# Row sums of attention 2's second head group: four key tiles added on VectorE and GpSimd, then multiplied with ones

## The chip, the cores and the metric

The kernel runs on one core of a Trainium2 chip. The metric is the device time of one execution in microseconds (us), lower is better. Engines as the profile names them: PE is TensorE (matmuls; PEld is its weight load), DVE is VectorE, ACT is ScalarE, POOL is GpSimd, SP is SyncE, which here only issues DMAs.

## The reference, cut to what matters

A batch of 16 sequences, T = 512 queries, width 256, context S = 1601 keys. Per sequence: a first cross attention with 16 heads and a layer norm, a Mamba block with its chunked scan, and a second cross attention with 8 heads of width 32:

```
q = (xn @ Wq).reshape(b, Lq, 8, 32);  k = (enc @ Wk)...;  v = (enc @ Wv)...
scores = einsum('bqhd,bkhd->bhqk', q, k) / sqrt(32)      # 8 heads x 512 queries x 1601 keys
p = softmax(where(pad_mask, -1e9, scores), axis=-1)
out = resid + einsum('bhqk,bkhd->bqhd', p, v) @ Wo
```

The kernel computes softmax as exp(score - maximum) and divides by the row sum at the end. The row sum of each query and head, over 1601 keys, is what the change touches.

## The kernel before

One loop over the 16 sequences, written out by hand for every engine; semaphores order the engines and each engine runs its instructions strictly in program order. Keys are cut into KT = 13 tiles of 128 (the last holds 65). Heads are taken in groups of GH = 4: attention 1 has G0 = 4 groups (gi = 0 to 3), attention 2 has G1 = 2 (gi = 4 and 5). In all texts "step t" is one round of the loop over t in `group`, "tile t" the key tile t.

In step t of a group of attention 2, TensorE computes the scores of tile t with keys on partitions: four matmuls of 512 columns (L1042), two heads ("half 0"), then two more ("half 1"). ScalarE takes the exponential of each half into `PR[:, t % 2]` (L1470; two buffers of four heads x 512 floats). Then `times_v` runs for tile t - 1: four matmuls that give each head 32 columns of the array, PR times V into PSUM bank 6 (L1067), and four of the same form that multiply PR with ones into bank 7 (L1072). The latter are the row sums, accumulated in PSUM over the 13 tiles. At the group's end ScalarE copies bank 7 to `rs` and bank 6 to `ctxn`; for the first group VectorE divides (`divide`) during step 0 of the second.

Between these matmuls TensorE takes entries of another piece of work, attention 1 of the next sequence: raw scores (L992, banks 4 and 5 in turn) that VectorE adds the mask to and reduces to a maximum (L1671, two instructions), and four projections of keys called "back" (L954), which ScalarE takes out (L1425 and L1428) ahead of its exponentials of the same step and GpSimd splits into three parts (L752, L755, L758). A table, `beside`, places the entries in six slots of a step: slots 0 to 3 behind the four score matmuls, slot 4 between V and the ones, slot 5 at the end. In the second group the four "back" entries are in slot 4 of steps 6 to 9. An entry's bank is free when VectorE (or ScalarE) is done with the entry two before it (`left`): TensorE waits for that in place. VectorE goes through the same slots in the same order. Raw entries of step 5 and later read `kst` and `qst`, which SP loads with 12 DMAs once the first group is done (L565, L568).

## Time and profile before

| | us |
|---|---|
| median of 3 runs | 8260.42 (8257.19 to 8279.29) |
| profiled execution, whole | 8254.75 |
| its span, first to last instruction | 8252.8 |
| TensorE busy | 7493.3 (91%) |
| VectorE busy | 5271.3 (64%) |
| ScalarE busy | 3415.3 (41%) |
| GpSimd busy | 1930.5 (23%) |
| matmuls with ones, L1072: 3328, busy | 444.4 |
| mean granted TensorE clock | 0.968 |

The table comes from the page of the profiled execution. Busy times are averages over stages that are limited by different engines, and a matmul's end is modelled: two matmuls that follow each other overlap in the rows, so what one costs TensorE is read from the distance between starts. The stretch from 3651 to 3718 us is the second head group of attention 2 in one of the 16 sequences.

### The profile page before, as it was taken

What the parts mean: (1) busy time and instruction counts of PE and PEld (TensorE: products, weight loads), DVE (VectorE), ACT (ScalarE), POOL (GpSimd) and SP (SyncE); (2) the same over time, 40 slices, a digit from 0 to 9 for tenths busy, and PEclk for the clock granted to TensorE, in tenths of its full rate; (3) what the DMA queues carried; (4) which work ended last, traced back from release to release, by engine and by line L of the source; (5) the groups of instructions that cost most, each with busy time, mean ns of one, the idle gap of its engine ahead of it and who ended that gap; (6) DMA issues with size and microseconds to landing.
All of it is one profiled execution on the core that took longest, in us unless ns stands there. A gap on an engine that the chain in (4) does not pass through costs nothing.

```text
span 8252.8 us, 130448 instructions
## 1 busy us (share of the span) xinstructions
PE 7493.3 (91%) x37924; PEld 3455.1 (42%) x38244; DVE 5271.3 (64%) x12637; ACT 3415.3 (41%) x4310; POOL 1930.5 (23%) x1928
## 2 busy tenths in 40 slices
PE   3999999999999999999999999999999999999999
PEld 0353443535334353443534335343343534435344
DVE  3676666766666675666765667666676666667656
ACT  0434435344353434535344353443534345343443
POOL 3041130402204031130401304022040311404113
PEclk6999999999999999999999999999999999999999
DMA  3142240423314142231422304233141322314223
GB/s 75 28 80 43 38 70 15 83 39 54 60 22 79 31 70 52 37 61 25 83 40 42 67 15 83 39 52 61 21 80 32 64 51 32 68 31 79 44 38 65
DMA packets 244583, 423.17 MB, mean 51 GB/s; under 512 B 38745, under 2 KB 154363, under 8 KB 243593
## 3 DMA queue, kind: packets, MB, share of 16 engines
q1 hardware_dynamic: 241751, 413.22, 29.0%
q8 instruction: 367, 6.01, 0.3%
q14 instruction: 417, 3.42, 0.1%
q10 hardware_dynamic: 2048, 0.53, 0.0%
HBM read 191.17 MB, written 8.54 MB: 24 GB/s over the span
## 4 chain that ended last, share of the span: by engine, by line
PE 73%; DVE 11%; issue 7%; ACT 4%; DMA 2%; SPq 1%; POOL 1%; DVEq 1%; ACTq 0%; POOLq 0%
PE ps L1067 13%; PE ps L992 11%; PE ps L954 8%; PE ps L1037 7%; PE ps L1040 6%; PE ps L1014 4%; DVE mx L1700 4%; PE ps L1072 4%; PE ps L1042 3%; ACT PR L1470 2%; PE ps L1222 2%; PE ps L1105 2%; PE ps L1278 2%; DVE ps L1735 1%; PE ps L1306 1%
## 5 line engine op out<-in xcount | busy, mean ns | idle before, releaser
L1470 ACT ACTIVATE PR<-ps 128x1024 f32<-128x1024 f32 x2496 | 2502.0, 1024 | 2449.1 <-PE ps L1040 1355.0
L1671 DVE CUSTOM_DVE_ANT_0 ps<-ps,maskq 128x402 f32<-128x402 f32 x4203 | 2405.6, 587 | 1452.1 <-PE ps L992 1320.1
L1067 PE MATMUL ps<-PR,vbuf 128*32 128x512 f32 x9984 | 1333.7, 606 | 7.5 <-ACT PR L1470 2.5
L992 PE MATMUL ps<-kst,qst 96*128 96x402 bf16 (+1 forms) x3115 | 1016.6, 340 | 126.1 <-DVE mx L1671 97.8
L1040 PE MATMUL ps<-maskk,identb 128*128 128x512 bf16 x2592 | 985.0, 380 | 0.0
L1700 DVE TENSOR_REDUCE mx<-ps 128x2 f32<-128x804 f32 x1024 | 932.8, 985 | 63.0 <-PE ps L1014 59.9
L1037 PE MATMUL ps<-qst,kst 99*128 99x512 bf16 x2496 | 916.8, 381 | 12.5 <-ACT PR L1470 5.2
L1014 PE MATMUL ps<-kst,qst 100*128 100x402 f32 x2688 | 733.1, 397 | 108.5 <-DVE mx L1700 107.7
L1042 PE MATMUL ps<-qst,kst 102*128 102x512 f32 x1664 | 728.3, 498 | 73.1 <-ACT PR L1470 70.8
L992 PEld LDWEIGHTS ps<-kst,qst 96*128 96x128 bf16 x3115 | 280.2, 97 | 1227.7 <-DVE mx L1671 856.0
L766 POOL MEMSET kst<- 96x252 f32 (+1 forms) x34 | 8.7, 255 | 3044.7 <-PE ps L1067 2997.8
L1014 PEld LDWEIGHTS ps<-kst,qst 100*128 100x128 f32 x2688 | 456.3, 194 | 367.0 <-DVE mx L1700 341.8
L1671 DVE DVE_READ_ACCUMULATOR2_ANT mx<- 128x1 f32 x4203 | 591.9, 141 | 0.0
L1735 DVE TENSOR_TENSOR ps<-ps,maskk 128x1024 f32<-128x1024 f32 x208 | 256.4, 1233 | 413.3 <-PE ps L1037 413.3
L727 POOL TENSOR_SCALAR maskk<-stage 128x512 bf16<-128x512 int32 (+1 forms) x238 | 428.5, 1801 | 330.4 <-DMA stage<-in_maskt 323.7
L992 PE MATMUL ps<-KS,QS 96*128 96x402 bf16 x1088 | 384.4, 354 | 112.0 <-DVE mx L1671 82.6
L954 PE MATMUL ps<-ctxs,wk_s 128*128 128x402 f32 (+1 forms) x1056 | 459.8, 562 | 24.7 <-ACT rest L1428 23.7
L727 POOL TENSOR_SCALAR maskq<-stage 128x402 bf16<-128x402 int32 (+1 forms) x272 | 427.8, 1573 | 192.4 <-DMA stage<-in_mask 169.6
L1072 PE MATMUL ps<-PR,ones 128*32 128x512 f32 x3328 | 444.4, 606 | 0.0
L1037 PEld LDWEIGHTS ps<-qst,kst 99*128 99x128 bf16 x2496 | 243.7, 98 | 416.6 <-ACT PR L1470 190.2
L1425 ACT ACTIVATE khl<-ps,cols 128x402 bf16<-128x402 f32 (+1 forms) x136 | 81.1, 596 | 796.7 <-PE ps L954 796.7
L954 PE MATMUL ps<-wv_s,ctxs 128*128 128x256 f32 (+1 forms) x1664 | 408.7, 380 | 0.0
(200 smaller groups left out, 8235.8 us busy)
## 6 DMA issues: line engine op xcount, KB each, us to landing
kst<-khl SPq DMA_DIRECT2D x300, 200.1 KB, 7.5
stage<-in_maskt SPq DMA_DIRECT2D x204, 256.0 KB
stage<-in_mask SPq DMA_DIRECT2D x204, 201.0 KB
kst<-khl SPq DMA_DIRECT2D x96, 402.0 KB, 8.6
kst<-khl SPq DMA_DIRECT2D x96, 398.5 KB, 11.1
ctxs<-in_ctxt SPq DMA_DIRECT2D x17, 1601.0 KB, 17.6
qst<-q1hl SPq DMA_DIRECT2D x192, 128.0 KB, 4.5
win_s<-in_w_in SPq DMA_DIRECT2D x16, 1288.0 KB, 5.7
```

Source lines behind the costliest of these rows:

```text
L727: nc.gpsimd.tensor_scalar(dst, stage[0:rows, n % 2, 0:w], 0.0, MASKED, ALU.is_equal, ALU.mult)\
L954: mm = pe.matmul(o, l, r, start=(k == 0), stop=(k == DT - 1))
L992: pe.matmul(ps[:, bank, 0:w], QS[gi][0:KROWS, h, i * P:(i + 1) * P], KS[gi][0:KROWS, h, c0:c0 + w], start=True, stop=True).then_inc(s_raw, 1)
L1014: mm = pe.matmul(ps[:, bank + e, 0:CW], QS1[g][0:MROW1 + 1, h, i * P:(i + 1) * P], KS1[g][0:MROW1 + 1, h, cc[e]:cc[e] + CW], start=True, s ...
L1037: mm = pe.matmul(o, KS[gi][0:SROWS, h, t * P:(t + 1) * P], QS[gi][0:SROWS, h, :], start=True, stop=(h in added))
L1040: mm = pe.matmul(o, identb[:, :], maskk[:, t, :], start=False, stop=True)
L1042: mm = pe.matmul(o, KS1[gi - G0][0:SROWS1, h, t * P:(t + 1) * P], QS1[gi - G0][0:SROWS1, h, :], start=True, stop=True)
L1067: mm = pe.matmul(ps[32 * j:32 * j + 32, 6, :], l, PR[:, t % 2, j, :], start=(t == 0), stop=(t == KT - 1), tile_position=(0, 32 * j))
L1072: mm = pe.matmul(ps[32 * j:32 * j + 32, 7, :], ones[:, 0:32], PR[:, t % 2, j, :], start=(t == 0), stop=(t == KT - 1), tile_position=(0, 32 ...
L1470: nc.scalar.activation(PR[:, t % 2, 2 * half:2 * half + 2, :], ps[:, bank:bank + 2, :], ACT.Exp, scale=scale).then_inc(s_p, 1)
L1671: nc.vector.tensor_tensor_reduce(src, src, maskq[:, i, c0:c0 + w], 1.0, -3.0e38, ALU.add, ALU.max, mx[:, c, h * QT + i:h * QT + i + 1]).th ...
L1700: nc.vector.tensor_reduce(mx[:, 2 * c:2 * c + 2, h * QT + i], ps[:, bank:bank + 2, 0:CW], AX.X, ALU.max)\
```

## The change

`SEGMENTS` tells for each head group of attention 2 over how many key tiles a sum is formed before it meets the ones. In the first group it is one tile each, as before. In the second it is 4, 4, 4 and 1: the probabilities of tiles 0 to 3 are added elementwise, those of tiles 4 to 7 and 8 to 11 too, and each sum is multiplied with ones once; tile 12 goes directly. So of 13 quads of L1072 in that group 4 remain. VectorE adds heads 0 and 1 (`add01`, one instruction of 128x1024 a tile, into `sum01`, part of `ctxn`), GpSimd adds heads 2 and 3 (`add23`, two instructions of 128x512 a tile, into `sum2` and `rs`). There are nine adds on each side, for tiles 1, 2, 3, 5, 6, 7, 9, 10 and 11; the first of a segment adds tiles t - 1 and t. ScalarE waits for the adds before it overwrites a buffer of PR. `add01` stands in slot 4 of step t on VectorE, `add23(t)` in a new loop over t on GpSimd in which the parts of the "back" entries of steps t + 1 and t + 2 follow the add of an odd t.

```diff
+        SEGMENTS = [[1] * KT, [4] * (KT // 4) + [1]]
...
 POOL
+                def add23(g, t):
+                    m = b * len(ADDS) + ADD_COUNT[g, t] - 1
+                    pool.wait_ge(s_p, b * 2 * NG * KT + ((G0 + g) * KT + t) * 2 + 2)
+                    if FIRST_ADD[g, t]:
+                        pool.wait_ge(s_addread, LEAD + b * len(ADDED) + sums_read(g, t))
+                        pool.wait_ge(s_norm, LEAD + b * NG + G0 + g)
+                    else:
+                        pool.wait_ge(s_add23, 2 * m)
+                    alone(pool)
+                    for j, dst in ((2, sum2[:, :]), (3, rs[:, :])):
+                        other = PR[:, (t - 1) % 2, j, :] if FIRST_ADD[g, t] else dst
+                        nc.gpsimd.tensor_tensor(dst, other, PR[:, t % 2, j, :], ALU.add).then_inc(s_add23, 1)
...
-                for item in BACK:
-                    parts(b + 1, item)
+                for t in range(KT):
+                    if (1, t) in ADD_COUNT:
+                        add23(1, t)
+                    for step in (t + 1, t + 2) if t % 2 else ():
+                        for j in BACK_STEPS.get(step, ()):
+                            parts(b + 1, BACK[j])
...
 PE, times_v
                 if gi >= G0:
+                    here = (gi - G0, t)
+                    if here not in DIRECT and t < KT - 1:
+                        mm.then_inc(s_pv, 1)
                     between(t + 1, 4)
-                    for j in range(GH):
-                        mm = pe.matmul(ps[32 * j:32 * j + 32, 7, :], ones[:, 0:32], PR[:, t % 2, j, :],
-                                       start=(t == 0), stop=(t == KT - 1), tile_position=(0, 32 * j))
-                mm.then_inc(s_pv, 1)
+                    if here in DIRECT:
...
+                    elif here in ADDED:
+                        assert t < KT - 1
+                        pe.wait_ge(s_add01, b * len(ADDS) + ADD_COUNT[here])
+                        pe.wait_ge(s_add23, 2 * (b * len(ADDS) + ADD_COUNT[here]))
+                        for j, src in enumerate((sum01[:, 0, :], sum01[:, 1, :], sum2[:, :], rs[:, :])):
+                            mm = pe.matmul(ps[32 * j:32 * j + 32, 7, :], ones[:, 0:32], src,
+                                           start=(here == ENDS_OF[gi - G0][0]), stop=False, tile_position=(0, 32 * j))
+                        mm.then_inc(s_addread, 1)
...
 ACT, exponentials
+                        if gi >= G0 and t >= 2:
+                            g = gi - G0
+                            read = adds_until(g, t - 1 if FIRST_ADD.get((g, t - 1)) else t - 2)
+                            if read and half == 0:
+                                act.wait_ge(s_add01, b * len(ADDS) + read)
+                            elif read:
+                                act.wait_ge(s_add23, 2 * (b * len(ADDS) + read))
...
 DVE
+            def add01(b, g, t):
+                dve.wait_ge(s_p, b * 2 * NG * KT + ((G0 + g) * KT + t) * 2 + 1)
+                if FIRST_ADD[g, t]:
+                    dve.wait_ge(s_addread, LEAD + b * len(ADDED) + sums_read(g, t))
+                    other = PR[:, (t - 1) % 2, 0:2, :]
+                else:
+                    dve.wait_ge(s_add01, b * len(ADDS) + ADD_COUNT[g, t] - 1)
+                    other = sum01
+                nc.vector.tensor_tensor(sum01, other, PR[:, t % 2, 0:2, :], ALU.add).then_inc(s_add01, 1)
...
+                        if slot == GH and (gi - G0, t) in ADD_COUNT:
+                            add01(b, gi - G0, t)
```

What moves in the order of the instructions is shown at three places. VectorE, second group, end of step 7 and start of step 8, before. "ISA ps,mx" and "ISA mx" together are one raw entry (mask and maximum); the 396 wide one is slot 0 of step 8:

```order
L1671 ISA ps,mx<-ps,maskq 128x402
L1671 ISA mx 128x1
L1659 REGISTER_ALU
L1671 ISA ps,mx<-ps,maskq 128x402
L1671 ISA mx 128x1
L1659 REGISTER_ALU
L1671 ISA ps,mx<-ps,maskq 128x396
L1671 ISA mx 128x1
```

The same place in the changed kernel:

```order
L1746 ISA ps,mx<-ps,maskq 128x402
L1746 ISA mx 128x1
L1805 REGISTER_ALU
L1810 REGISTER_ALU
L1812 TENSOR_TENSOR ctxn<-ctxn,PR 128x1024
L1734 REGISTER_ALU
L1746 ISA ps,mx<-ps,maskq 128x402
L1746 ISA mx 128x1
L1734 REGISTER_ALU
L1746 ISA ps,mx<-ps,maskq 128x396
L1746 ISA mx 128x1
```

The add of tile 7, with its two waits, now stands between the entry of slot 3 and that of slot 5.

TensorE, end of step 8 (V of tile 7, the third "back" projection, the sums, slot 5), before:

```order
L1067 MATMUL ps<-PR,vbuf 32x512 x4
L968 REGISTER_ALU
L954 MATMUL ps<-ctxs,wk_s 128x402 x2
L1072 MATMUL ps<-PR,ones 32x512 x4
L968 REGISTER_ALU
L992 MATMUL ps<-kst,qst 128x396
```

and in the changed kernel (sum_61 is `sum2`):

```order
L1120 MATMUL ps<-PR,vbuf 32x512 x4
L1021 REGISTER_ALU
L1007 MATMUL ps<-ctxs,wk_s 128x402 x2
L1135 REGISTER_ALU
L1136 REGISTER_ALU
L1138 MATMUL ps<-ctxn,ones 32x512 x2
L1138 MATMUL ps<-sum_61,ones 32x512
L1138 MATMUL ps<-rs,ones 32x512
L1021 REGISTER_ALU
L1045 MATMUL ps<-kst,qst 128x396
```

The four matmuls with ones stay here, but now behind waits for VectorE's and GpSimd's sums; in steps 1, 2, 3, 5, 6, 7, 9, 10 and 11 they are gone.

GpSimd, second group, behind the parts of the fourth "back" entry (395 wide), before:

```order
L755 CAST khl<-rest 128x395
L756 REGISTER_ALU
L758 TENSOR_TENSOR khl<-rest,khl 128x395
L918 ISA
L762 MEMSET kst 96x4x63
```

and in the changed kernel:

```order
L783 CAST khl<-rest 128x395
L784 REGISTER_ALU
L786 TENSOR_TENSOR khl<-rest,khl 128x395
L941 REGISTER_ALU
L943 REGISTER_ALU
L950 TENSOR_TENSOR sum_61<-PR 128x512
L950 TENSOR_TENSOR rs<-PR 128x512
L941 REGISTER_ALU
L946 ISA
L950 TENSOR_TENSOR sum_61<-sum_61,PR 128x512
L950 TENSOR_TENSOR rs<-rs,PR 128x512
```

The adds of tiles 9, 10 and 11 follow the last parts; those of tiles 6 and 7 stand in the same way behind the parts of the second "back" entry, ahead of those of the third.

## Rows read from the trace of the kernel before

**Rows 1.** Page, part 1: busy us (share of the span) xinstructions
```profile
PE 7493.3 (91%) x37924; PEld 3455.1 (42%) x38244; DVE 5271.3 (64%) x12637; ACT 3415.3 (41%) x4310; POOL 1930.5 (23%) x1928
```
**Rows 2.** Timeline of PE (start us, us, ..., idle before <-releaser), steps 1 and 5
```profile
3655.88 1.04 PE L1072 MATMUL ps<-PR,ones 128*32 128x512 f32 x8
3656.85 0.50 PE L1042 MATMUL ps<-qst,kst 102*128 102x512 f32 x1
...
3667.76 0.34 PE L992 MATMUL ps<-kst,qst 96*128 96x402 bf16 x1 [0.52 <-DMA qst<-qhl]
```
**Rows 3.** Source view, L992: what its engine waited for (us, times)
```profile
  DMA qst<-qhl: 6.5, 11
```
**Rows 4.** Timeline of PE, steps 7 and 8 of the second group
```profile
3682.71 1.62 PE L954 MATMUL ps<-ctxs,wk_s 128*128 128x402 f32 x4
3684.26 1.07 PE L1072 MATMUL ps<-PR,ones 128*32 128x512 f32 x8
...
3686.42 0.51 PE L1042 MATMUL ps<-qst,kst 102*128 102x512 f32 x1 [0.81 <-ACT PR L1470]
...
3687.18 0.34 PE L992 MATMUL ps<-kst,qst 96*128 96x402 bf16 x1
...
3688.76 1.07 PE L1067 MATMUL ps<-PR,vbuf 128*32 128x512 f32 x8
3689.75 1.62 PE L954 MATMUL ps<-ctxs,wk_s 128*128 128x402 f32 x4
```
**Rows 5.** Timeline of ACT, step 7
```profile
3684.37 0.60 ACT L1425 ACTIVATE khl<-ps,cols 128x402 bf16<-128x402 f32 x1 [4.12 <-PE ps L954]
...
3685.34 1.94 ACT L1470 ACTIVATE PR<-ps 128x1024 f32<-128x1024 f32 x2
```
**Rows 6.** Waits of the whole span: us, times, longest
```profile
PE ps L1042 <- ACT PR L1470: 70.8, 96, 1.0
```
**Rows 7.** Windows: us, busy of each engine (x), PEclk, DMA share, GB/s
```profile
3681.00:3688.00 7.00, 6.06 (x31) 2.03 (x31) 3.04 (x11) 2.91 (x4) 2.34 (x4) 1.00 0.00 1
3702.00:3707.00 5.00, 4.79 (x28) 1.59 (x28) 3.71 (x13) 2.36 (x3) 0.26 (x1) 1.00 0.68 101
...
3564.00:3568.00 4.00, 2.75 (x10) 1.26 (x9) 3.93 (x7) 1.08 (x2) 3.71 (x3) 1.00 0.20 51
3568.00:3572.00 4.00, 3.77 (x10) 2.29 (x9) 4.00 (x5) 0.00 (x0) 3.69 (x4) 0.52 0.20 54
```
**Rows 8.** Timeline of DVE, steps 0, 7, 10 and 11
```profile
3655.92 0.69 DVE L1726 TENSOR_TENSOR ctxn<-ctxn,rs 128x512 f32<-128x512 f32 x1
...
3685.75 0.58 DVE L1671 CUSTOM_DVE_ANT_0 ps<-ps,maskq 128x402 f32<-128x402 f32 x1 [3.08 <-PE ps L992]
...
3704.31 0.58 DVE L1671 CUSTOM_DVE_ANT_0 ps<-ps,maskq 128x402 f32<-128x402 f32 x1 [0.63 <-PE ps L992]
...
3709.23 0.58 DVE L1671 CUSTOM_DVE_ANT_0 ps<-ps,maskq 128x396 f32<-128x396 f32 x1 [0.63 <-PE ps L992]
```
**Rows 9.** Timeline of DVE, two operations with both operands in SBUF, in the Mamba block
```profile
3457.52 2.38 DVE L1840 SCALAR_TENSOR_TENSOR xc<-th,xc 128x512 f32<-128x512 f32 x1
...
3497.00 1.21 DVE L1860 TENSOR_TENSOR windows<-windows,GM 128x1024 f32<-128x1024 f32 x1
...
3501.05 0.69 DVE L1917 TENSOR_TENSOR ug<-ug,zs 128x512 f32<-128x512 f32 x1
```
**Rows 10.** Timeline of POOL at the same places
```profile
3457.01 2.34 POOL L829 TENSOR_TENSOR aU<-aa,upto 128x1024 f32<-128x1024 f32 x1
...
3497.24 1.87 POOL L857 TENSOR_TENSOR dx<-dx,dec 128x512 f32<-128x512 f32 x1 [4.13 <-DVE dx L1895]
3499.07 1.04 POOL L864 TENSOR_TENSOR Hst<-Hst,dec 128x512 f32<-128x512 f32 x1
```
**Rows 11.** Timeline of POOL, step 7 of the second group
```profile
3685.60 0.90 POOL L752 TENSOR_TENSOR rest<-rest,khl 128x402 f32<-128x402 f32 x1 [4.38 <-ACT rest L1428]
3686.62 0.52 POOL L755 CAST khl<-rest 128x402 bf16<-128x402 f32 x1
3687.29 0.95 POOL L758 TENSOR_TENSOR khl<-rest,khl 128x402 bf16<-128x402 f32 x1
```

More of the change, by code:

```diff
@@ L474, in xattn_mamba, with adds_until, sums_read @@
         NMX = 4
+        SEGMENTS = [[1] * KT, [4] * (KT // 4) + [1]]
+        assert all(sum(x) == KT for x in SEGMENTS)
+        ADDS, ENDS = [], []
+        for g, lengths in enumerate(SEGMENTS):
+            t = 0
+            for n in lengths:
+                ADDS += [(g, t + i, i == 1) for i in range(1, n)]
+                t += n
+                ENDS.append((g, t - 1, n > 1))
+        ADD_COUNT = {(g, t): n + 1 for n, (g, t, _) in enumerate(ADDS)}
+        FIRST_ADD = {(g, t): is_first for g, t, is_first in ADDS}
+        ENDS_OF = [[(h, t) for h, t, _ in ENDS if h == g] for g in range(G1)]
+        ADDED = [(g, t) for g, t, several in ENDS if several]
+        DIRECT = [(g, t) for g, t, several in ENDS if not several]
+        def adds_until(g, t):
+            return max([ADD_COUNT[x] for x in ADD_COUNT if x[0] == g and x[1] <= t], default=0)
+        def sums_read(g, t):
+            return sum(x < (g, t) for x in ADDED)
         def head_bank(gi, t, half):
@@ L909, in _ @@
                     n += 1
+                def add23(g, t):
[11 more added lines that the diff above has]
+                for t in range(KT):
+                    if (0, t) in ADD_COUNT:
+                        add23(0, t)
+                    if t % 2:
+                        for n in range(n, min(n + 2, NPIECE)):
+                            piece(n)
+                        n = min(n + 1, NPIECE)
                 for n in range(n, NPIECE):
@@ L1162, in whole_decays @@
                 mm.then_inc(s_dps, 1)
-            for first in (s_pv, s_yp):
+            for first in (s_pv, s_yp, s_addread):
                 pe.nop(nofuse=True).then_inc(first, LEAD)
```

14 lines of the change are left out of this document (added).

## The prediction

> **What bounds the kernel now.** I read the page first, then the timeline of each engine over the second head group of attention 2 (3651 to 3718 us), then the waits and windows. The page makes TensorE look like the bound: busy 91% of the span, the next engine 64% [rows 1]. By that, a quad of ones that disappears is a pure gain. A quad costs TensorE the distance from its start to the next matmul's, 3656.85 - 3655.88 = 0.97 us [rows 2]. Nine quads a sequence and 16 sequences give 9 x 0.97 x 16 = 140 us, the most that the change can bring. So the question is which of those nine places TensorE really sets. The reader is to see three kinds of steps.
>
> Steps 0 to 4 are short and end in a DMA: the first raw entry of step 5 starts at 3667.76 after 0.52 us of idle time that a load of `qst` ended [rows 2]. The same wait stands in 11 of the 16 sequences, 6.5 us in all, with the same size each [rows 3]. That load depends on the end of the first group, not on this one, so TensorE arriving earlier only waits longer.
>
> Steps 6 to 9 hold a "back" projection. In step 7 it starts at 3682.71 [rows 4]; ScalarE can take it out only when it is done, at 3684.37, and its exponential of half 0 starts at 3685.34 [rows 5]; the scores of step 8 need that and start at 3686.42, after 0.81 us of idle time on TensorE [rows 4]. The quad of ones (3684.26 to about 3685.3) lies beside ScalarE's part. From one projection to the next it is 7.04 us (3682.71 to 3689.75) [rows 4]. Such waits of scores for ScalarE occur 96 times, six a sequence, 70.8 us [rows 6].
>
> Steps 10 to 12 look bound by TensorE (4.79 us busy of 5.00), but VectorE is busy 3.71 us there [rows 7]. A step is 3709.23 - 3704.31 = 4.92 us [rows 8]; VectorE has 4.92 - 3.71 = 1.21 us left.
>
> **Durations of the added work.** VectorE's add, 128x1024 with both operands in SBUF: 1.21 us, from the same form in the Mamba block [rows 9]. GpSimd's, 128x512: 1.04 us with nothing beside it [rows 10]; two of them and the wait ahead of them, 2.2 us a tile. Beside each other they aren't independent. GpSimd's L857, of the same 128x512 as L864, takes 1.87 instead of 1.04 us: it starts at 3497.24 while VectorE's L1860 runs until 3498.21, and 1.87 - 1.04 = 0.83 is nearly what was left of it [rows 9, 10]. The other way round, VectorE's L1840 takes 2.38 us (a 128x512 with two operands in SBUF takes 0.69): it starts at 3457.52, in the middle of a GpSimd operation that ends at 3459.35 [rows 9, 10]. So I let whoever comes second wait for the instruction of the first. The Trainium skill says the same (SBUF — State Buffer, "Who interferes with whom"): a VectorE instruction with two SBUF inputs contends with a GpSimd instruction that reads SBUF, and the second blocks fully. The trace agrees; without that rule my sum below would be 62 us, with it 92.
>
> **The change, place by place** (one sequence; then times 16).
>
> Removed quads. Tiles 0, 1, 2 (steps 1 to 3): 0, the DMA takes it. Tiles 5, 6, 8 (steps 6, 7, 9): 0, they lay beside ScalarE's 2 us. Tiles 4, 9, 10 (steps 5, 10, 11): TensorE saves 0.97 a step, but VectorE gets 1.21 more in the same step and has 1.21 left, so the raw entries, each of which waits for VectorE's entry two before, go on at the old pace of about 4.9 us: 0, between -0.1 and +0.1 each.
>
> Adds, steps 1 to 4: +0.4. VectorE's add of tile 1 comes after the division (ends 3656.61 [rows 8]) and ends at 3657.8; GpSimd's pair waits for the same division and then for that add, so it runs to 3660.0. ScalarE may overwrite the buffer only then; its half 1 of step 2 ends at 3661.1. The pair of tile 2 follows with VectorE's add of tile 3 between its two halves (61.2 to 64.5), then tile 3 (64.6 to 66.7). TensorE's first quad of sums runs until 67.8, and the first raw entry of step 5 comes at 68.2 instead of 67.76. Bounds: 0 (the adds never meet) to 1.5 (each GpSimd add costs 1.87).
>
> Adds in "back" steps: +1.15 each for tiles 6, 7 and 9, together 3.45. This is the largest term. VectorE's add stands ahead of slot 5's entry and waits for the exponential of its tile. In step 7 that ends just ahead of the scores it releases, about 3686.4 [rows 4], while slot 5's entry was done by 3686.4, from 3685.75 on [rows 8]. Now the add runs from 3686.4, behind GpSimd's L752 that ends at 3686.50 [rows 11], to 3687.7, the entry until 3688.35. The raw entry of slot 1 in step 8 needs that entry's bank: it started at 3687.18 [rows 4] and now starts at 3688.4. All that is queued behind it moves: two score matmuls, V, the next projection, which sets the chain of the next step. VectorE idled there before (3.08 us ahead of slot 5's entry [rows 8]), but the idle time is ahead of the exponential and the add can't use it. Bounds: 0 to 1.3 each.
>
> The sums in step 8: +0.5. GpSimd splits the second projection first (3685.60 to 3688.24 [rows 11], +1.15 for the shift, +1.1 for VectorE's add in between: 3690.5), then adds tiles 6 and 7 (4.4 us: 3694.95). TensorE, 2.3 us later than before, is through with its third projection at 3693.6, waits 1.4 us, and the quad and slot 5's entry end at 3696.25; ScalarE would have released the next scores at 3695.75. Bounds 0 to 1.5.
>
> VectorE behind GpSimd in steps 10 and 11: +0.9 and +0.5. GpSimd's adds of tiles 9, 10 and 11 come in one row after the fourth projection's parts; VectorE's add of tile 10 meets the second half of tile 9's (0.9), that of tile 11 perhaps one more (half of 1.04). VectorE has nothing left there, so it counts. Bounds 0 to 2.2 together.
>
> Sum: 0.4 + 3.45 + 0.5 + 1.4 = 5.75 us a sequence, times 16 = 92 us. Against the profiled execution's 8254.75 us (span 8252.8, 2 us around it) that is 8347; the median of the runs lies 6 us above the profiled one. I say 8350. The low bounds (only the "back" steps at 0.85, nothing else) give 41 us, 8296; the high ones 1.5 + 3.9 + 1.5 + 2.2 = 9.1, 146 us, 8400.
>
> **Rivals.**
>
> A. TensorE is the bound after all. The savings in steps 1 to 3, 5, 10 and 11 count, 6 x 0.97 = 5.8 us, and the adds find VectorE idle: 16 x 5.8 = 93 us less, 8160. For it: the 91%, and VectorE's idle time of 1.21 us a step. Against it: the DMA's 0.52 us, which decides the first three, and the place of the add behind the exponential. It decides from the point at which the add ends before the entry of slot 1 is asked for; the numbers miss that by 1.2 us three times a sequence.
>
> B. The adds hide better than I think, for instance because TensorE had 0.81 us of slack in each "back" step that takes part of the shift: 3 x 0.4 + 0.5 = 1.7 us, 27 us, 8282. Against it: the stall is on the far side of that slack, behind the scores' start.
>
> C. TensorE's clock falls. In this group the granted clock is 1.00 with TensorE busy 6.06 of 7.00 us [rows 7]. Elsewhere it fell to 0.52 right after four microseconds with 2.75 us busy, 69% [rows 7]. In steps 6 to 9 the changed kernel leaves 0.81 + 0.97 + 1.15 = 2.9 us idle of 8.2, 65% busy, in two gaps close together; steps 1 to 4 have a gap of 2 us too. A stretch at 1.2 GHz instead of 2.4 GHz over half a step's 5 us of matmuls costs about 2.5 us; once or twice a sequence 40 to 80 us on top: 8390 to 8430. The Trainium skill (TensorE: Matmul & The Clock Gate, "What's actually happening") says that activity alone releases the throttle, and so speaks against a change that takes matmuls away; no row here shows this group below 1.00.
>
> **How the numbers follow.** Forecast 0.62, C 0.22, B 0.07, A 0.05, and no visible change 0.04 (every term near its low bound). A measurement of this kernel tells about 0.3%, 25 us, from no change. Faster: A, 0.05, and a little of the rest, 0.06. Same: 0.04 and a part of B, 0.06. Slower 0.88. Range: from the low bounds to the middle of C, 8295 to 8415; that leaves out A, part of B and the upper half of C.
>
> **What the profile of the changed kernel would show.** Right: the ones quads of this group at 4 x 16 instead of 13 x 16; the first raw entry of step 5 still about where the load of `qst` puts it; from one "back" projection to the next 8.2 us instead of 7.04 behind steps 6 and 7; in steps 7, 8 and 10 raw entries of slot 1 waiting more than 1 us for VectorE; waits of TensorE for GpSimd's sums once in step 8; VectorE's adds longer than 1.21 us where GpSimd runs; the group 5 to 7 us longer than 66; all else unchanged. Wrong: step 5 starting 3 us earlier (A), slot 1's entry without a wait (B), a granted clock of 0.5 in the group (C).

## The result, and the profile after

The changed kernel takes 8400.80 us, median of 4 runs (8399.85 to 8401.66); the kernel before, run beside it on the same chip, 8258.81 (8249.94 to 8279.29, 4 runs). The ratio is 1.0168, 95% interval 1.0149 to 1.0187: 142 us more, 8.9 us a sequence. The forecast was 92 us more, 8350, with a range of 8295 to 8415. Direction and range hold; the size does not.

The page of the changed kernel, span and part 1 (as [rows 1]):

```profile
span 8399.9 us, 130033 instructions
PE 7541.8 (90%) x37092; PEld 3464.3 (41%) x37092; DVE 5482.3 (65%) x12781; ACT 3413.7 (41%) x4310; POOL 2381.8 (28%) x2216
```

TensorE has 832 matmul records fewer: 1152 with ones are gone, as the change has it, and 320 more stand for the mask matmuls of attention 1 (`maskk,identb`), which the change leaves alone and of which the record of before lacks some. So the 48.5 us more of busy time can't be taken as they are; without the mask matmuls in both they are 17.5 us. Even that is more time for fewer matmuls. Its mean granted clock, the share of full speed that the chip let it run at, went from 0.968 to 0.946. The lines of the kernel that answer for the change, with the shortest, the median and the longest of one instruction in ns (the ones over single tiles that stay, then VectorE's adds, then two of GpSimd's four groups of adds):

```profile
L1129 PE MATMUL ps<-PR,ones x1792: 592/592/617, 605.1 to 8389.3; 128*32 128x512 f32 x200
...
L1812 DVE TENSOR_TENSOR ctxn<-ctxn,PR x96: 1218/1429/2225, 662.9 to 8381.5; 128x1024 f32<-128x1024 f32 x96
...
L950 POOL TENSOR_TENSOR sum<-sum,PR x96: 1259/1276/2084, 665.3 to 8381.7; 128x512 f32<-128x512 f32 x96
...
L950 POOL TENSOR_TENSOR sum<-PR x48: 1262/2062/2120, 660.6 to 8373.8; 128x512 f32<-128x512 f32 x48
```

The diff asks for 9 x 16 = 144 adds of VectorE and twice as many of GpSimd; the rows above are 96 of the former and half of the latter. Their shortest are 1.22 and 1.26 us.

The timeline of TensorE over steps 6 to 8 of one sequence's second group, where [rows 4] showed 7.04 us from one projection to the next:

```profile
3742.64 1.87 PE L1120 MATMUL ps<-PR,vbuf 128*32 128x512 f32 x8
3744.44 2.47 PE L1007 MATMUL ps<-ctxs,wk_s 128*128 128x402 f32 x4
...
3748.99 0.50 PE L1095 MATMUL ps<-qst,kst 102*128 102x512 f32 x1 [1.91 <-ACT PR L1545]
...
3750.89 0.51 PE L1045 MATMUL ps<-kst,qst 96*128 96x396 bf16 x1 [0.82 <-DVE mx L1746]
...
3752.91 1.94 PE L1120 MATMUL ps<-PR,vbuf 128*32 128x512 f32 x8
3754.77 2.42 PE L1007 MATMUL ps<-ctxs,wk_s 128*128 128x402 f32 x4
...
3765.07 2.39 PE L1007 MATMUL ps<-ctxs,wk_s 128*128 128x402 f32 x4
```

The reader is to see three things. From projection to projection it is 3754.77 - 3744.44 = 10.33 us, then 10.30. Where a wait of 0.81 us for ScalarE stood, it is 1.91: the 0.97 of the removed quad has become idle time of about its length, not a shorter step. And the matmuls themselves are longer: those of V take 1.87 to 1.94 us where they took 1.07, the projection 2.4 to 2.5 where it took 1.62. The windows over the same steps and over steps 10 to 12 say why (busy of each engine, then the granted clock):

```profile
3744.00:3755.00 11.00, 8.26 (x26) 2.95 (x23) 4.24 (x11) 2.91 (x4) 3.25 (x3) 0.66 0.00 1
3755.00:3765.00 10.00, 7.30 (x21) 2.44 (x21) 4.24 (x11) 2.91 (x4) 5.84 (x6) 0.67 0.00 0
3765.00:3773.00 8.00, 7.13 (x34) 2.59 (x31) 2.98 (x10) 2.91 (x4) 4.77 (x5) 0.90 0.00 1
3784.00:3796.00 12.00, 10.15 (x67) 3.02 (x66) 8.32 (x27) 5.18 (x6) 5.08 (x5) 1.00 0.84 94
```

The clock is 0.66 of full in step 6, so it stood at 1.2 GHz for about two thirds of that stretch, against 1.00 in [rows 7]. This was rival C. The Trainium skill (TensorE: Matmul & The Clock Gate, "What's actually happening") says that activity releases the throttle; this trace agrees, with 1.00 before and 0.66 after nine quads were taken away and the waits for the adds put in.

VectorE and GpSimd, first two adds of the group and the add of step 6, each engine's timeline:

```profile
3722.79 1.22 DVE L1812 TENSOR_TENSOR ctxn<-PR 128x1024 f32<-128x1024 f32 x1
...
3725.28 2.18 DVE L1812 TENSOR_TENSOR ctxn<-ctxn,PR 128x1024 f32<-128x1024 f32 x1 [0.71 <-ACT PR L1545]
...
3749.06 1.23 DVE L1812 TENSOR_TENSOR ctxn<-ctxn,PR 128x1024 f32<-128x1024 f32 x1 [5.56 <-ACT PR L1545]
3750.20 0.58 DVE L1746 CUSTOM_DVE_ANT_0 ps<-ps,maskq 128x402 f32<-128x402 f32 x1
```
```profile
3723.02 2.11 POOL L950 TENSOR_TENSOR sum<-PR 128x512 f32<-128x512 f32 x1 [4.76 <-DVE ctxn L1801]
3725.11 1.26 POOL L950 TENSOR_TENSOR rs<-PR 128x512 f32<-128x512 f32 x1
```

In step 6 the add waits 5.56 us for the exponential, then runs 1.23 us, and slot 5's entry starts only at 3750.20; TensorE's entry of slot 1, at 3750.89, is behind it. So VectorE's idle time is of no use to the add, as forecast. The first rows show the two engines in each other's way. The waits that these leave in the whole span (us, times, longest):

```profile
PE ps L1045 <- DVE mx L1746: 213.2, 510, 45.2
...
PE ps L1095 <- ACT PR L1545: 146.9, 120, 1.9
```

The second was 70.8 us in 96 waits [rows 6]; the first, in the kernel before:

```profile
PE ps L992 <- DVE mx L1671: 180.4, 469, 45.2
```

All of the loss is in the second group. The table below is worked out from the timelines: the distance from one V (the weighted sum of a key tile) to the next, mean of the 16 sequences, in us; column 6 is the distance that ends at V of tile 6, and column 0 counts from the last V of the first group. "1.2 GHz" is the time in the group at the lower clock level. The clock falls in some sequences and not in others, so a column can also be read where it stood at 1.00 throughout; texts below say "with the clock up" for that. The first group, attention 1 and the blocks between stay within about 1 us a sequence in the changed kernel. Names of the experiments are those used further down.

```
                   0    1    2    3    4    5    6     7    8    9    10   11   12   group  1.2 GHz
before           5.61 3.66 3.58 3.16 4.70 4.92 7.04  7.04 7.04 7.01 4.92 4.92 2.54  66.16    1.1
after            5.60 2.31 4.85 3.45 6.04 4.54 9.06  9.65 8.53 8.39 5.44 4.62 3.04  75.52   24.3
fill             5.62 3.45 3.93 3.16 5.34 4.93 8.23  8.95 8.59 7.95 5.65 4.92 2.54  73.27    7.0
adds_only        5.64 3.33 3.95 3.16 5.41 4.93 8.20  9.14 8.65 7.95 5.53 4.93 2.54  73.35    6.4
quads_only       5.61 2.68 2.48 2.30 7.97 5.18 7.46  8.50 7.44 7.63 4.75 4.18 2.54  68.73   16.0
quads_back       5.62 3.86 3.58 3.16 4.62 4.93 7.48  8.37 8.21 7.67 5.19 4.92 2.54  70.14   11.5
pool_only        5.60 3.15 3.57 3.14 4.87 4.91 7.03  7.03 9.53 7.01 4.91 4.91 2.54  68.22    3.0
dve_only         5.65 3.83 3.57 3.16 4.56 4.91 8.30  8.46 8.28 8.05 6.00 4.91 2.54  72.23    8.8
seg_mid          5.60 3.16 3.58 3.16 4.91 4.55 8.53 10.30 8.79 7.01 4.93 4.93 2.54  71.99   13.2
late             5.62 2.96 4.76 2.68 9.40 4.91 7.24  7.10 9.07 7.44 6.63 4.93 3.34  76.08   17.9
late_order_fill  5.62 3.55 4.92 3.26 8.76 5.35 7.04  7.13 7.13 7.01 6.69 5.16 3.35  74.96    8.3
mix_fill         5.63 3.65 3.87 3.16 5.22 4.93 7.04  7.03 7.86 7.02 8.83 6.20 2.54  72.99    9.6
mix              5.68 3.35 3.78 2.64 6.87 4.85 7.64  8.02 8.15 7.44 8.44 5.19 2.54  74.60   24.1
first_group      5.60 3.16 3.58 3.16 9.61 6.06 7.05  7.42 7.03 7.00 4.92 4.92 2.54  72.07    7.7
```

### The profile page after: what moved, and what is told of

Read it like the earlier page. It is cut to its first block, busy times and chain, and to the rows that moved or that the text cites. A ratio compares the mean times of both kernels' runs of the same rounds, so it can differ in the third digit from the quotient of the medians.

```text
span 8399.9 us, 130033 instructions
## 1 busy us (share of the span) xinstructions
PE 7541.8 (90%) x37092; PEld 3464.3 (41%) x37092; DVE 5482.3 (65%) x12781; ACT 3413.7 (41%) x4310; POOL 2381.8 (28%) x2216
## 4 chain that ended last, share of the span: by engine, by line
PE 73%; DVE 12%; issue 8%; ACT 3%; POOL 1%; DVEq 1%; DMA 1%; SPq 0%; ACTq 0%; POOLq 0%
PE ps L1120 13%; PE ps L1045 11%; PE ps L1007 8%; PE ps L1090 7%; PE ps L1093 6%; PE ps L1067 5%; DVE mx L1775 4%; PE ps L1095 4%; PE ps L1129 3%; ACT PR L1545 2%; PE ps L1290 2%; PE ps L1173 2%; PE ps L1346 2%; PE ps L1374 1%; DVE ps L1821 1%
## 5 line engine op out<-in xcount | busy, mean ns | idle before, releaser
L1120 PE MATMUL ps<-PR,vbuf 128*32 128x512 f32 x9984 | 1394.4, 632 | 7.4 <-ACT PR L1545 2.5
L1045 PE MATMUL ps<-kst,qst 96*128 96x402 bf16 (+1 forms) x3115 | 1041.8, 351 | 142.1 <-DVE mx L1746 130.3
L1093 PE MATMUL ps<-maskk,identb 128*128 128x512 bf16 x2912 | 1106.5, 380 | 0.0
L1095 PE MATMUL ps<-qst,kst 102*128 102x512 f32 x1664 | 788.0, 534 | 149.8 <-ACT PR L1545 146.9
L1007 PE MATMUL ps<-ctxs,wk_s 128*128 128x402 f32 (+1 forms) x1056 | 484.6, 588 | 23.2 <-ACT rest L1496 22.2
L1095 PEld LDWEIGHTS ps<-qst,kst 102*128 102x128 f32 x1664 | 332.3, 208 | 317.4 <-ACT PR L1545 235.3
## 6 DMA issues: line engine op xcount, KB each, us to landing
ctxs<-in_ctxt SPq DMA_DIRECT2D x17, 1601.0 KB, 17.5
```

The lines of the kernel that those rows point to most:

```text
L1007: mm = pe.matmul(o, l, r, start=(k == 0), stop=(k == DT - 1))
L1045: pe.matmul(ps[:, bank, 0:w], QS[gi][0:KROWS, h, i * P:(i + 1) * P], KS[gi][0:KROWS, h, c0:c0 + w], start=True, stop=True).then_inc(s_raw, 1)
L1093: mm = pe.matmul(o, identb[:, :], maskk[:, t, :], start=False, stop=True)
L1095: mm = pe.matmul(o, KS1[gi - G0][0:SROWS1, h, t * P:(t + 1) * P], QS1[gi - G0][0:SROWS1, h, :], start=True, stop=True)
L1120: mm = pe.matmul(ps[32 * j:32 * j + 32, 6, :], l, PR[:, t % 2, j, :], start=(t == 0), stop=(t == KT - 1), tile_position=(0, 32 * j))
```

## Experiments

Two theories stood against each other after the result. The add theory: all of the loss comes from the adds and their waits, and the removed quads are worth nothing. The clock theory: part of it comes because TensorE's work went away. Times are medians; "before" is the kernel before, measured beside each; ratios carry their 95% interval.

### fill: quads with zero weights where the quads of ones went

```
+                    elif t in range(KT):
+                        for j in range(GH):
+                            pe.matmul(ps[32 * j:32 * j + 32, 7, :], zeros[:, :], PR[:, t % 2, j, :],
+                                      start=(t == 0), stop=False, tile_position=(0, 32 * j))
```

> The changed kernel, and in the place of each of the nine removed quads of ones a quad with weights of zero over the same tile of PR, so that TensorE does as many matmuls as before; every wait and every add stays. Theory 1 (stalls: VectorE's add ahead of slot 5's entry, GpSimd's sums late in step 8, adds behind each other) gives 5.75 us a sequence with the clock at 1.00 in this group. Theory 2 (the clock, which fell in this group in every sequence of the changed kernel, makes up the rest of the measured 8.9 us a sequence) expects this kernel to be FASTER than the changed one although it does more: 8259 + 92 = 8350 us, 8340 to 8365, mean clock back near 0.968. If the clock is only a companion of the stalls, the quads cost nothing or something: 8400 or more, clock 0.95.

8368.21 (8363.56 to 8371.58, 4 runs) against before 8256.43 (9 runs): 1.0135 (1.0118 to 1.0152). Nine more quads a sequence than the changed kernel, and 32.6 us faster; the slowest of its runs is 28 us below the fastest of the changed kernel's, and the intervals of the two ratios only just touch (1.0149 and 1.0152). Time at 1.2 GHz in the group fell from 24.3 to 7.0 us a sequence. TensorE, steps 6 to 9 of one sequence:

```profile
3736.75 0.34 PE L1047 MATMUL ps<-kst,qst 96*128 96x396 bf16 x1 [0.98 <-DVE mx L1752]
...
3747.65 1.87 PE L1122 MATMUL ps<-PR,vbuf 128*32 128x512 f32 x8
3749.45 2.46 PE L1009 MATMUL ps<-ctxs,wk_s 128*128 128x402 f32 x4
...
3752.19 0.62 PE L1140 MATMUL ps<-ctxn,ones 128*32 128x512 f32 x2 [0.28 <-POOL rs L952]
...
3756.34 1.06 PE L1122 MATMUL ps<-PR,vbuf 128*32 128x512 f32 x8
...
3762.82 0.34 PE L1047 MATMUL ps<-kst,qst 96*128 96x402 bf16 x1 [0.90 <-DVE mx L1752]
...
3764.28 1.06 PE L1122 MATMUL ps<-PR,vbuf 128*32 128x512 f32 x8
```

The measured 8368 lies just above the expected 8340 to 8365. The raw entry behind an add waits 0.90 to 0.98 us, and where the clock stays up the step is 3764.28 - 3756.34 = 7.94 us, 0.9 more than 7.01. In step 8 of this sequence V of tile 7 and the projection behind it take 1.87 and 2.46 us, at 1.2 GHz; TensorE then comes late to GpSimd's sums and waits only 0.28 us for them.

### adds_only: adds and waits stay, all 13 quads of ones stay too, the sums are not used

```
-                        for j, src in enumerate((sum01[:, 0, :], sum01[:, 1, :], sum2[:, :], rs[:, :])):
-                            mm = pe.matmul(..., ones[:, 0:32], src, ...)
+                        for j in range(GH):
+                            mm = pe.matmul(..., ones[:, 0:32], PR[:, t % 2, j, :], ...)
```

> Adds and all their waits as in the changed kernel, but the row sums of the second group by 13 quads of ones over PR as before (the sums of four tiles are formed and not used; TensorE still waits for them in steps 4, 8 and 12). Theory 1 and 2 together: the stalls alone, clock kept, about 8350 us, and within 15 us of the kernel with zero weights, since both keep 13 quads. If instead the removed quads had brought something in steps 5, 10 and 11 (0.97 us each), the difference between this and before would be larger, up to 8259 + 16 x (5.75 + 2.9) = 8397.

8374.43 (8371.85 to 8375.74, 4 runs): 1.0144 (1.0127 to 1.0161), the same as fill step by step in the table. That the filling quads have zero weights is not what helps; that TensorE has the work is. It is above the expected 8350 and within 15 us of fill, as expected.

This run also shows what the adds and waits cost with the clock up, since in one sequence the clock stays at 1.00 from step 2 to the group's end. Step 8 there, TensorE's timeline and the window:

```profile
699.62 1.06 PE L1120 MATMUL ps<-PR,vbuf 128*32 128x512 f32 x8
...
704.43 1.06 PE L1138 MATMUL ps<-PR,ones 128*32 128x512 f32 x8 [2.20 <-POOL rs L950]
...
708.08 1.06 PE L1120 MATMUL ps<-PR,vbuf 128*32 128x512 f32 x8
```
```profile
699.62:708.08 8.46, 5.98 (x31) 1.98 (x30) 2.99 (x11) 2.91 (x4) 6.65 (x7) 1.00 0.01 3
```

TensorE waits 2.20 us for GpSimd and the step takes 8.46 us, 1.42 more than 7.04. In 13 of the other 14 sequences, with 3.4 us at 1.2 GHz, it takes 8.7: the slower matmuls stand where the wait stood. The other columns with the clock up are 8.06, 8.07 and 7.95 (6, 7 and 9), 26.39 for columns 0 to 5 together against 25.36 before, and 13.00 for 10 to 12 against 12.39; fill has the same values wherever its clock stays up, which it never does in column 8.

### quads_only: the same nine quads go from the kernel before, nothing is added

Row sums of nine tiles are left out.

```
+                    keep = gi == G0 or t % 4 == 3 or t == KT - 1
-                    for j in range(GH):
+                    for j in range(GH) if keep else ():
```

> The kernel before with the quads of ones of tiles 0-2, 4-6 and 8-10 of the second group left out, nothing added; the row sums of that group then miss those tiles. Theory 1: steps 1-3 end in the load, steps 6, 7 and 9 in ScalarE; steps 5, 10 and 11 have VectorE busy only 3.71 of 4.92 us, so there the quads do pay without the adds: up to 3 x 0.97 us a sequence, 8259 - 47 = 8212 us. Theory 2 takes from that what the lower clock costs in steps 6 to 9, where TensorE then idles 1.8 us of 7: V, back projection and scores at 1.2 GHz add about 2 us to each step that is hit, so 8212 to 8300. The rival that TensorE sets the steps: 9 x 0.97 x 16 = 140 us less, 8120.

8310.57 (8289.08 to 8317.55, 4 runs): 1.0057 (1.0038 to 1.0077), above the 8212 to 8300 of the theory with the clock. Less work and nothing in its place, and the kernel is slower by 54 us. Waits of the whole span:

```profile
PE ps L992 <- DMA qst<-qhl: 46.6, 16, 3.3
```

Columns 1 to 3 are 2.9 us shorter and column 4 is 3.3 longer: TensorE comes early and waits for the load of `qst`, in all 16 sequences. That is the DMA claim of the prediction. Columns 6 to 9 grow by 2.9 us together with no add anywhere; they have 7.6 of the group's 16.0 us of low clock, and where the clock stays up they take 7.04 or less, as before. Columns 10 to 12 are 0.9 us shorter, 1.5 with the clock up: there the removed quads do pay.

### quads_back: only the three quads of tiles 5, 6 and 8 go

Their row sums are left out.

```
+                    keep = gi == G0 or t not in (5, 6, 8)
```

> The kernel before with three quads of ones left out, those of tiles 5, 6 and 8 (steps 6, 7 and 9 of the second group); nothing is added, and the row sums of that group miss these tiles. Place-by-place theory without the clock: the three quads lie beside ScalarE, so the time stays 8255, within 10 us. Theory with the clock: with TensorE idle 1.8 us instead of 0.8 in each of these steps the granted clock falls to 1.2 GHz in some of them, and what is left of the work takes twice as long there: 1 to 2 us a sequence SLOWER by removing work, 8270 to 8290. Rival (TensorE sets the steps): 3 x 0.97 x 16 = 47 us faster, 8208.

8349.42 (8330.93 to 8354.93, 5 runs) against 8266.45 (8250.8 to 8289.92, 9 runs): 1.0091 (1.0072 to 1.0109). Three quads a sequence that lay beside ScalarE's work were left out, and it costs 83 us, more than expected, and more than quads_only lost with nine. Windows of one sequence, the end of step 4 to step 8:

```profile
4237.00:4247.00 10.00, 9.57 (x55) 3.22 (x54) 6.16 (x24) 3.99 (x4) 0.00 (x0) 1.00 0.07 8
4247.00:4254.00 7.00, 4.97 (x21) 1.88 (x21) 2.92 (x11) 2.92 (x4) 2.36 (x3) 0.98 0.01 2
4254.00:4263.00 9.00, 7.09 (x22) 2.61 (x21) 3.09 (x10) 2.91 (x4) 2.36 (x3) 0.69 0.00 1
4263.00:4272.00 9.00, 8.06 (x31) 2.62 (x29) 2.96 (x11) 2.91 (x4) 2.33 (x3) 0.76 0.00 0
```

At a clock of 0.98 the 7 us of step 6 hold 4.97 us of work, and the step takes 7.3: little is lost yet. Then the clock is 0.69, the same matmuls need 7.09 us, and the step takes 9.3. Of the 6.3 us a sequence that this profiled execution is longer than that of before, 4.0 lie in the group, 64 us in all; the other 2.3 lie in the stretches around it, where nothing was changed. They can't be put down to the quads: the profiled executions of the other kernels differ from that of before by -18 to +32 us in the same unchanged stretches, this one by +37.

### pool_only and dve_only: one engine's adds at a time

In each, two of the four heads are added as in the change and the other two meet the ones tile by tile. The cores of the edits:

```
pool_only
-                            add01(b, gi - G0, t)
+                        for j in range(2):
+                            pe.matmul(..., ones[:, 0:32], PR[:, t % 2, j, :], ...)
dve_only
-                    if (1, t) in ADD_COUNT:
-                        add23(1, t)
+                        for j in (2, 3):
+                            pe.matmul(..., ones[:, 0:32], PR[:, t % 2, j, :], ...)
```

> Only GpSimd adds (heads 2 and 3, with all its waits); heads 0 and 1 meet the ones tile by tile, two matmuls in each step, which take as long as four since the four run side by side. VectorE's adds are gone. Theory 1: the three stalls of 1.15 us and the meetings of the two engines go; left is TensorE's wait for the sums in step 8, 1.2 to 1.5 us a sequence with GpSimd's adds at 1.27 us: 8259 + 22 = 8281 us, 8265 to 8290, clock near 0.968. If GpSimd's adds and its place behind the projections' parts were the main cost, 8340 or more.

> Only VectorE adds (heads 0 and 1, with all its waits); heads 2 and 3 meet the ones tile by tile, so TensorE has two matmuls in each step, as long as four; GpSimd's adds are gone. Theory: the wait of slot 1's raw entry in steps 7, 8 and 10 (V6, V7, V9 late by 1.15 to 1.2 us each) stays, the wait of step 8 for GpSimd and the meetings go: 3.5 us a sequence, 8255 + 56 = 8311 us, 8295 to 8330. With the one for GpSimd alone (2.5 us a sequence, 43 us) this should add up to about the 112 us of the kernel with zero weights. Rival: the two need each other, each alone costs little: 8280.

GpSimd's alone: 8299.37 (8289.01 to 8324.35, 6 runs), 1.0058 (1.004 to 1.0075), more than the expected 8265 to 8290. VectorE's alone: 8369.52 (8358.52 to 8388.48, 4 runs), 1.0124 (1.0101 to 1.0147), more than expected. GpSimd costs one place: column 8 grows by 2.5 us, since TensorE waits for the sums there,

```profile
3716.76 0.63 PE L1137 MATMUL ps<-PR,ones 128*32 128x512 f32 x2 [2.30 <-POOL rs L950]
```

and columns 6, 7 and 9 are as before, although half of each quad went. In 14 of the 16 sequences the clock falls in column 8 as well; in the two others the column is 8.55, so 1.5 us are the wait and the rest is the clock. With VectorE's adds columns 6 to 10 grow by 1.3, 1.4, 1.2, 1.0 and 1.1. Columns 8 and 10 do so by the clock alone: where it stays up they are 7.04 (one sequence) and 4.91 (five), as before, against 8.06, 8.07 and 7.94 for columns 6, 7 and 9. V of tile 7, which begins column 8, takes 1.94 us in one of the others:

```profile
3741.88 1.94 PE L1116 MATMUL ps<-PR,vbuf 128*32 128x512 f32 x8
```

So in step 8 a wait for GpSimd with the clock up, or TensorE at 1.2 GHz, each make the step longer, and with both it is hardly longer than with one (8.46 and 8.7 us in adds_only).

### seg_mid: one segment of four, tiles 4 to 7, the rest direct

```
-        SEGMENTS = [[1] * KT, [4] * (KT // 4) + [1]]
+        SEGMENTS = [[1] * KT, [1] * 4 + [4] + [1] * 5]
```

> The second group's segments are 1,1,1,1,4,1,1,1,1,1: only tiles 4 to 7 are added, on both engines; the other nine tiles meet the ones directly, so steps 0 to 4 and 10 to 12 are as before. Theory (place by place): the steps up to the third 'back' projection carry most of the cost: V6, V7 and V8 late by 1.2, 1.2 to 1.9 and 1.5 us, plus the clock, which can fall since three quads are missing in steps 5 to 7: 4 to 6 us a sequence, 8257 + 80 = 8337 us, 8320 to 8355. Rival (the cost is spread evenly over the nine adds): 3/9 of 144 us, 8305.

8336.95 (8329.85 to 8350.5, 4 runs) against 8253.65 (7 runs): 1.0112 (1.0069 to 1.0154). Three adds instead of nine, and 83 us of the 142 are there; columns 6 to 8 take 6.5 us more, all others together 0.7 less. The number that was expected, 8337, came, but in part by luck: columns 6, 7 and 8 are late by 1.5, 3.3 and 1.8 us where 1.2, 1.2 to 1.9 and 1.5 were expected with the clock to come on top, and the profiled execution is 18 us shorter than that of before in stretches that were not changed.

### late: VectorE adds tile t in the next step

The add no longer stands between the exponential and the entry of slot 5.

```
-                        if slot == GH and (gi - G0, t) in ADD_COUNT:
-                            add01(b, gi - G0, t)
+                        if slot == GH and (gi - G0, t - 1) in ADD_COUNT:
+                            add01(b, gi - G0, t - 1)
```

> The changed kernel with VectorE's add of tile t moved one step on, to slot 4 of step t + 1, where VectorE is idle before ScalarE's exponential; all else as in the changed kernel. Theory 1: the wait of slot 1's raw entry for VectorE in steps 7, 8 and 10 goes (1.15 us each, 3.45 a sequence, 55 us); the clock still falls, since the quads are still missing: 8401 - 55 = 8346 us, 8325 to 8370. If the place of the add isn't what costs: 8395 or more.

8440.81 (8418.97 to 8446.11, 4 runs): 1.0227 (1.0182 to 1.0272). It missed the expected 8346 by almost 100 us. Columns 6 and 7 did fall back to 7.24 and 7.10. But the sums of step 4 now come late (column 4: 9.40).

### late_order_fill: the same, GpSimd's parts ahead of its adds, zero quads

```
+                    for j in BACK_STEPS.get(t, ()):
+                        parts(b + 1, BACK[j])
                     if (1, t) in ADD_COUNT:
                         add23(1, t)
```

> As the kernel with the late add, and two more edits: zero-weight quads keep TensorE's work (clock), and GpSimd splits a 'back' projection in its own step and adds that step's tile right behind it (before, the adds of tiles 6 and 7 stood behind the parts of the second projection). All three costs that I name are taken away while every add stays; only what steps 1 to 4 lose and what VectorE lacks in steps 10 and 11 is left: 0.8 + 0.7 us a sequence in the kernel with zero weights, 24 us: 8257 + 24 = 8281 us, 8262 to 8300. If the three causes don't exhaust the cost, it stays above 8320.

8413.31 (8405.82 to 8418.62, 4 runs): 1.0196 (1.0153 to 1.0238), against 8281 expected, again a miss. Columns 6 to 9 are 7.01 to 7.13, as before: an add away from that place costs those steps nothing. What it costs is ahead of them. VectorE and TensorE in step 4:

```profile
4245.37 2.22 DVE L1817 TENSOR_TENSOR ctxn<-ctxn,PR 128x1024 f32<-128x1024 f32 x1
...
4248.80 1.19 DVE L1721 SCALAR_TENSOR_TENSOR mrest<-mxr,nm 128x16 f32<-128x16 f32 x1
...
4250.42 1.23 DVE L1817 TENSOR_TENSOR ctxn<-ctxn,PR 128x1024 f32<-128x1024 f32 x1
```
```profile
4251.78 1.07 PE L1139 MATMUL ps<-ctxn,ones 128*32 128x512 f32 x2 [2.90 <-DVE ctxn L1817]
```

Tile 3's add is queued behind the computation of the group's maxima, of which one operation of 0.18 us takes 1.19 behind GpSimd, and TensorE stands still for 2.90 us at the sums.

### mix_fill and mix: late adds only for tiles 5, 6, 7 and 9, with and without zero quads

```
+                            for u in (t - 1, t):
+                                if (gi - G0, u) in ADD_COUNT and (u < t) == (u in (5, 6, 7, 9)):
+                                    add01(b, gi - G0, u)
```

> All adds on both engines; VectorE's adds of tiles 5, 6, 7 and 9 in slot 4 of the step after, the others in their own step; GpSimd splits a 'back' projection in its own step, then adds; zero-weight quads keep TensorE's work. From the steps measured in the two kernels it joins: V0 to V4 as with zero weights (21.5 us), V5 to V9 as with the late add (about 33.3), V10 to V12 about 13.4: 68.2 us for the group against 66.16 before, 2 us a sequence, 8255 + 33 = 8288 us, 8272 to 8305. If the late adds only moved their cost to another place, 8340 or more.

> The same without the zero-weight quads: the changed kernel's work with the adds placed where they do not stop the raw entries. If the removed quads pay once the stalls are gone: below 8255 + 33 = 8288 us and perhaps at 8255. With the clock theory: the quads' absence lets the clock fall in steps 6 to 9, as in the kernel with quads left out and nothing added (54 us slower than before): 8310 to 8345, slower than with zero-weight quads.

mix_fill: 8367.58 (8364.79 to 8371.02, 4 runs), 1.012 (1.0101 to 1.0139), expected 8288. mix: 8406.11 (8378.17 to 8421.93, 4 runs), 1.0155 (1.0131 to 1.018), expected 8310 to 8345. In mix_fill columns 6, 7 and 9 are 7.02 to 7.04 again and the cost has moved to column 10 (8.83), where tile 9's late add and tile 10's own now meet in one slot:

```profile
4268.82 2.27 DVE L1817 TENSOR_TENSOR ctxn<-PR 128x1024 f32<-128x1024 f32 x1
...
4272.34 1.23 DVE L1817 TENSOR_TENSOR ctxn<-ctxn,PR 128x1024 f32<-128x1024 f32 x1 [1.26 <-ACT PR L1550]
```
```profile
4271.20 1.94 ACT L1550 ACTIVATE PR<-ps 128x1024 f32<-128x1024 f32 x2 [4.58 <-DVE ctxn L1817]
```
```profile
4272.28 0.50 PE L1096 MATMUL ps<-qst,kst 102*128 102x512 f32 x1 [1.56 <-ACT PR L1550]
...
4274.18 0.52 PE L1046 MATMUL ps<-kst,qst 96*128 96x396 bf16 x1 [1.40 <-DVE mx L1751]
```

ScalarE may not overwrite the buffer that the first of the adds still reads. The pair repeats the test of fill in another schedule: without the zero quads 38.5 us more, and 24.1 instead of 9.6 us a sequence at 1.2 GHz. Here the two intervals overlap a little, and of the 38.5 us 26 lie in the group.

### first_group: the segments in the first head group, the second direct

```
-        SEGMENTS = [[1] * KT, [4] * (KT // 4) + [1]]
+        SEGMENTS = [[4] * (KT // 4) + [1], [1] * KT]
```

> Segments 4,4,4,1 in the first head group of attention 2 and 1 x 13 in the second. There TensorE is busy 57.9 of 60 us, VectorE 41, GpSimd 25 (mask conversions that wait for their DMAs), and no 'back' projection makes a chain with ScalarE. Theory: there TensorE sets the steps, so nine quads of 0.97 us would save 8.7 us a sequence, but VectorE gets 11 us more on 41 of then 51: it becomes the bound at 52 to 53 us, and GpSimd's adds (2.5 us a tile) stand between mask conversions of 1.9 us. I expect half the gain at most: 4 us a sequence, 8257 - 64 = 8193 us, 8160 to 8280; with the clock falling there too, up to 8330.

8414.46 (8407.05 to 8416.21, 4 runs): 1.0198 (1.0156 to 1.024), where 8193 was expected, a gain. Column 4 is 9.61, in a group that was not touched:

```profile
PE ps L1045 <- DMA qst<-qhl: 71.3, 16, 4.7
```

The load of `qst` that [rows 3] showed in 11 short waits is now the bound in each sequence. GpSimd's queue and SP's, one sequence, tell why:

```profile
4243.59 1.07 POOL L755 TENSOR_SCALAR maskk<-stage 65x256 bf16<-65x256 int32 x1 [0.99 <-DMA stage<-in_maskt]
4244.71 0.55 POOL L790 MEMSET kst<- 96x252 bf16 x2
```
```profile
4245.10 4.87 SPq L593 DMA_DIRECT2D kst<-khl  x6
```

GpSimd is through with the mask conversions only at 4244.66, after its adds; the memset that the loads wait for comes behind them, and SP issues the loads 0.4 us after its start. That is 6.8 us after the first group's last V, where it was 2.4 us in a sequence of the kernel before. The first group itself takes 51.86 us instead of 49.39.

No version beat the kernel before.

## Why the prediction was right in direction and low in size

In us a sequence, the terms as predicted, as measured with the quads in place and the clock up (from the sequences of adds_only and of before whose clock stays at 1.00 in the columns asked for), as measured in fill, and as measured in the changed kernel (the last two are differences of the table's means; columns 0 to 5 together are "steps to 5"):

```
term                       predicted  clock up   fill    after
steps to 5                    +0.4     +1.03    +0.80   +1.16
add of tile 6 (column 6)      +1.15    +1.02    +1.19   +2.02
add of tile 7 (column 7)      +1.15    +1.03    +1.91   +2.61
sums in step 8 (column 8)     +0.5     +1.42    +1.55   +1.49
add of tile 9 (column 9)      +1.15    +0.94    +0.94   +1.38
columns 10 to 12              +1.4     +0.61    +0.73   +0.72
sum                           +5.75    +6.05    +7.12   +9.38
```

So the adds and their waits were sized almost right in sum, 97 us for 92; that is partly luck, since the terms that came out larger (steps to 5, step 8) and those that came out smaller make up for each other. What the forecast left out is the clock. No single sequence has the clock up in all 13 columns; the column is put together from several.

**The removed quads: the step that failed.** The prediction said "0, the DMA takes it" and "0, they lay beside ScalarE's 2 us". Both halves of the reason are right: quads_only shows the DMA's wait grow to 3.3 us, and the step of 7 us in quads_back is not shortened. But 0 is the wrong worth. A quad that lies in TensorE's waiting keeps the engine busy, and without it the clock falls. In place of 0 the runs show a loss: 32.6 us by after against fill, 38.5 us by mix against mix_fill, 54 us by nine quads alone, 83 us by three (in the group itself 36, 26, 41 and 64 us). These are net of what the quads save where the clock stays up, and this was put at 0 as well: step 5 and step 11 are 0.4 and 0.3 us shorter in the changed kernel than in fill. The prediction had this as rival C at 0.22; it is the case that came, and 8400.8 is inside its 8390 to 8430. Of the 9.38 us a sequence, 3.3 are beyond the adds with the clock up; 1.1 of them are there in fill too, whose quads are in place. The row that spoke for it was there: 0.52 after four microseconds with 69% busy [rows 7].

**The adds in the steps with a projection: right in place and nearly in size.** 0.94 to 1.03 us with the clock up, against 1.15. The experiments with late adds show the place to be the cause: with the add elsewhere those columns return to 7.04. What column 7 has more than that in fill is the clock: it is 8.07 in the two sequences with the clock up, and 9.0 to 9.3 where 2.2 to 2.7 us of it were at 1.2 GHz.

**The sums in step 8: right in kind, low in size.** TensorE was to wait 1.4 us for GpSimd, for a net 0.5; with the clock up it waits 2.20 us, for a net 1.42. GpSimd's four adds of tiles 6 and 7 take 5.4 us there, from 698.97 to 704.38, against 4.4 in the forecast. In fill and in the changed kernel the clock hides this wait and costs as much in its place: 0.28 us of waiting, with 1.87 and 2.46 us for V and the projection.

**Steps 10 and 11: half.** +0.6 to +0.7 instead of +1.4. VectorE's adds of tiles 10 and 11 in fill:

```profile
3765.00 2.21 DVE L1818 TENSOR_TENSOR ctxn<-ctxn,PR 128x1024 f32<-128x1024 f32 x1
...
3770.53 1.22 DVE L1818 TENSOR_TENSOR ctxn<-ctxn,PR 128x1024 f32<-128x1024 f32 x1
```

The first meets GpSimd's second half of tile 9, 0.99 us for a forecast of 0.9; the second meets nothing.

**Steps 1 to 4: right in kind, low.** +1.0 with the clock up instead of +0.4, within its bound of 1.5. GpSimd's add is 1.26 us, not 1.04: the row chosen had another form, and six adds in the first segment carry 0.22 each.

**Who comes second waits for the first: right.** GpSimd's first add takes 2.11 us beside VectorE's, 0.85 more, and VectorE's second takes 2.18, 0.96 more, with 1.09 of GpSimd's left when it starts. The Trainium skill (SBUF — State Buffer, "Who interferes with whom") has the second one fully blocked; the trace agrees, within 0.15 us.

**Rival A, TensorE as the bound, is out.** Fewer matmuls made it slower in each run that tells it apart. Only steps 5, 10 and 11 pay for a removed quad, and too little. Rival B is out by the 0.9 to 1.0 us that each add of tiles 6, 7 and 9 costs with the clock up.

**Three quads cost more than nine, and why.** Of the 1.4 us a sequence between quads_back and quads_only in the group, 1.2 come from columns 10 to 12, where quads_only saves 0.9 us by quads that quads_back still has. Of its longer time at 1.2 GHz (16.0 us against 11.5) 6.0 us fall in columns 4 and 5, where TensorE waits for the load anyway. In columns 6 to 9 quads_back has more of it, 9.4 us against 7.6, and loses more, 3.6 us against 2.9.

**Open.** Why the clock falls in one sequence of a kernel and stays up in the next, at the same step with the same matmuls. In fill, whose quads are in place, the waits behind the adds are the likely reason for its 7.0 us at 1.2 GHz; no run tests that.

## What to carry to other kernels

A matmul engine that is 91% busy need not be the bound: look at what ends each step, and price a removed matmul at the wait that it lay in, then ask what the clock does when that wait is twice as long. Work that fills a wait of TensorE can be worth more than its removal. An add that needs the newest result of another engine costs nearly its full length (here 0.94 to 1.03 of 1.22 us) when it is queued ahead of an entry that someone waits for, whatever the idle time of its engine; moving it freed that place here and cost as much elsewhere, at the next user of its sum and at the engine that wanted its buffer back, so look at those two first.
